# A two-layer cross-attention kernel: the turned context comes from memory instead of from TensorE, and its lower part from GpSimd

## The reference, cut to what matters

```python
# layer 0, for each of the 32 batches
q = Wq y + bq;  k = Wk y + bk;  v = Wv x + bv          # 128 x 1024 each
scores = einsum('bhdl,bhel->bhde', q, k) / sqrt(E)     # 16 x 16 per head
o = Wo (softmax(scores) v) + bo + x
x1 = (o - mean(o)) * rsqrt(var(o) + eps) * gn_w + gn_b
# layer 1: hidden_states = x1, traces = y
q = x1 @ W'q;  k = y @ W'k;  v = y @ W'v               # W' = W + 2 A B
out = x1 + softmax(q k^T / sqrt(32)) v @ W'o           # 32 query heads, 8 key heads
```

## Time and profile before

| | |
|---|---|
| median of 3 runs | 1332.63 us (1332.49 to 1335.76) |
| span of the profiled execution, which is taken for its own time | 1332.9 us |
| TensorE busy | 1321.9 us (99% of the span) |
| VectorE, ScalarE, GpSimd busy | 927.1, 826.5, 150.4 us |
| TensorE's transposes of y (L523) | 256, 34.1 us busy |
| granted TensorE clock | 1.000 |

### The profile page before, as it was taken

The page is one execution under the profiler, slowest core; times in us unless marked ns, Lnnn a source line. Parts: engine busy times, 40 slices in busy tenths (PEclk is TensorE's granted clock), DMA queues, the critical chain, the costliest instruction groups (busy, mean ns, idle before and its releaser), DMA issues.

```text
span 1332.9 us, 23820 instructions
## 1 busy us (share of the span) xinstructions
PE 1321.9 (99%) x7171; PEld 1055.4 (79%) x7171; DVE 927.1 (70%) x2080; ACT 826.5 (62%) x2934; POOL 150.4 (11%) x124
## 2 busy tenths in 40 slices
PE   8999999999999999999999999999999999999999
PEld 7888888888888888888888888766776777766667
DVE  6766666666666777777767776597777677666666
ACT  5766665555541777777757776666666666655441
POOL 5343333222210000000000001400000000000000
PEclk9999999999999999999999999999999999999999
DMA  7466566667757888777778888999999899988882
GB/s 220 147 209 207 202 201 210 221 218 222 241 164 220 232 228 232 226 237 226 222 215 230 228 239 260 271 253 252 264 253 251 247 248 263 256 220 232 235 227 88
DMA packets 194961, 300.42 MB, mean 225 GB/s; under 512 B 26578, under 2 KB 94004, under 8 KB 194324
## 3 DMA queue, kind: packets, MB, share of 16 engines
q1 hardware_dynamic: 194836, 298.90, 77.9%
HBM read 213.88 MB, written 84.93 MB: 224 GB/s over the span
## 4 chain that ended last, share of the span: by engine, by line
PE 95%; DVE 2%; DMA 1%; SPq 1%; issue 1%; ACT 1%; DVEq 0%; ACTq 0%
PE bank L707 26%; PE bank L757 23%; PE bank L586 13%; PE bank L778 8%; PE bank L811 5%; PE bank L822 5%; PE bank L660 3%; PE bank L523 2%; PE bank L572 2%; PE bank L678 2%; PE bank L614 1%; PE bank L693 1%; PE bank L619 1%; PE bank L545 1%; PE bank L633 1%
## 5 line engine op out<-in xcount | busy, mean ns | idle before, releaser
L1058 ACT ACTIVATE bank<-bank,negs 128x128 f32<-128x128 f32 x1024 | 348.3, 341 | 174.8 <-DVE negs L1340 174.4
L707 PE MATMUL bank<-hT,wq 128*128 128x512 f32 x1488 | 390.2, 400 | 0.0
L757 PE MATMUL bank<-wo,op 128*128 128x512 f32 (+1 forms) x1356 | 346.0, 393 | 0.3 <-issue 0.3
L707 PEld LDWEIGHTS bank<-hT,wq 128*128 128x128 f32 x1488 | 264.0, 189 | 46.2
L757 PEld LDWEIGHTS bank<-wo,op 128*128 128x128 f32 x1356 | 249.6, 189 | 52.0 <-issue 1.5
L1335 DVE TENSOR_REDUCE maxes<-bank 128x4 f32<-128x512 f32 x256 | 175.8, 687 | 134.2 <-PE bank L778 134.2
L1075 ACT ACTIVATE probT<-bank 128x512 f32<-128x512 f32 x256 | 152.2, 605 | 112.9 <-PE bank L811 110.1
L1058 ACT ACTIVATION_READ_ACCUMULATOR bank<-bank,negs 128x1 f32 x1024 | 210.0, 205 | 0.0
L586 PE MATMUL bank<-wkv_hi,yT 128*128 128x512 f32 x512 | 200.3, 420 | 0.9 <-DVE wkv_lo L1487 0.7
L778 PEld LDWEIGHTS bank<-k_stack,q_stack 96*128 96x128 f32 x1024 | 150.3, 191 | 17.5 <-issue 1.6
L778 PE MATMUL bank<-k_stack,q_stack 96*128 96x128 f32 x1024 | 147.3, 266 | 1.0 <-issue 0.6
(11 more groups left out here) (172 smaller groups left out, 1629.5 us busy)
## 6 DMA issues: line engine op xcount, KB each, us to landing
q_stack<-q_dram SPq DMA_DIRECT2D x256, 256.0 KB, 4.0
q_dram<-q_part SPq DMA_DIRECT2D x64, 512.0 KB, 4.2
q_stack<-q_dram SPq DMA_DIRECT2D x256, 128.0 KB, 4.3
y_in<-in_ctx SPq DMA_DIRECT2D x32, 512.0 KB, 4.5
x_in<-in_x SPq DMA_DIRECT2D x32, 512.0 KB, 5.1
h_dram<-h_out SPq DMA_DIRECT2D x32, 512.0 KB, 2.7
h_in<-h_dram SPq DMA_DIRECT2D x32, 512.0 KB, 3.9
k_stack<-k_dram SPq DMA_DIRECT2D x128, 128.0 KB, 3.4
```

The source lines that it names most:

```text
L707: m = pe.matmul(bank(u % 2).rearrange("p (a n) -> p a n", a=2), wq[:, block, part, c, :], hT[(group + 1) % 2][:, :, of, c, :], start=c == ...
L757: mm = pe.matmul(place[:, columns], op[m][:, of, c, :], wo[m][w][:, c, columns], start=c == 0 and of == 0 and w == 0, stop=c == GROUP - 1 ...
L1058: act.activation(part, part, ACT.Exp, bias=negs[:, n % RING, j:j + 1], scale=SCORE1, accum_out=sums[:, score_column(k), g, j:j + 1]).then_ ...
```

## The change

The host lays out a second copy of the context, `ctx_turned`, in which the positions of each chunk lie on the partitions. SyncE loads it into `yT_in` (`load_yT`, 512 KB a batch), beside the untouched one, which is still needed for the sums. `turn_y` goes, with its 256 transposes. ScalarE rounds the whole of `yT_in` in one instruction out of SBUF. The lower part of batches 0 and 1 is still made by VectorE (`rest_yT`, now with both inputs in SBUF); that of batches 2 to 31 by GpSimd (`lower_yT(b + 1)` in turn b, 128x1024, both inputs in SBUF, behind the power). TensorE's idle transposes at the start (`keep_on`) become 26 in one piece, and small products on rows of the identity.

```diff
-            def turn_y(b):
-                ...
-                for c in range(NC):
-                    m = pe.transpose(banks[0][:, c * P:(c + 1) * P], y_in[b % 2][:, c * P:(c + 1) * P], ident[:])
+            def wait_yT(b, half):
+                if b < 2:
+                    pe.wait_ge(S["yT_lo"], 2 * b + half + 1)
                 else:
-                    pe.wait_ge(S["const"], CONST["ident"])
+                    pe.wait_ge(S["yT_lo_pool"], b - 1)
...
-            def round_yT(b, half):
+            def round_yT(b, half=None):
...
-                act.wait_ge(S["yT_mm"], 2 * b + half + 1)
-                act.copy(yT_half(b, half, 0), bank(half).rearrange("p (c n) -> p c n", c=4)).then_inc(S["yT_hi"], 1)
+                act.wait_ge(S[f"yT_in{b % 2}"], DMA * (b // 2 + 1))
+                of = yT_chunks(half)
+                act.copy(yT[b % 2][:, of, 0, :], yT_in[b % 2][:, of, :]).then_inc(S["yT_hi"], 1)
...
-                dve.tensor_tensor(yT_half(b, half, 1), bank(half).rearrange("p (c n) -> p c n", c=4),
-                                  f32(yT_half(b, half, 0)), ALU.subtract).then_inc(S["yT_lo"], 1)
+                dve.tensor_tensor(yT[b][:, of, 1, :], yT_in[b][:, of, :], f32(yT[b][:, of, 0, :]),
+                                  ALU.subtract).then_inc(S["yT_lo"], 1)
...
                 norm_scale(b - 1)
-                rest_yT(b + 1, 0)
                 softmax0_end(b)
...
-                rest_yT(b + 1, 1)
...
+            def lower_yT(b):
+                if b >= B:
+                    return
+                pool.wait_ge(S["yT_hi"], 4 + b - 1)
+                pool.tensor_tensor(yT[b % 2][:, :, 1, :], yT_in[b % 2][:], f32(yT[b % 2][:, :, 0, :]),
+                                   ALU.subtract).then_inc(S["yT_lo_pool"], 1)
...
                 if b == 1:
                     stack_lora("o")
+                lower_yT(b + 1)
                 for n in units_of(b)[:-1]:
                     prep_rest(n)
...
             for b in range(B):
+                load_yT(b + 2)
+                load_x(b + 1)
                 load_y(b + 2)
-                load_x(b + 1)
```

More of the change, by code:

```diff
@@ L133, in xattn_two_layers @@
         lora_raw("o")
+        yT_in = [sb(f"yT_in{i}", [P, NC, P]) for i in range(2)]
         at[0] = w_place
@@ L502, in op_part, with yT_chunks @@
             return op[m][:, part, :, :].rearrange("p j n -> p (j n)")
-        def yT_half(b, half, part):
-            return yT[b % 2][:, 4 * half:4 * half + 4, part, :]
+        def yT_chunks(half):
+            return slice(0, NC) if half is None else slice(4 * half, 4 * half + 4)
         def tensor_program(pe):
@@ L673, in turn_h @@
                     pe.wait_ge(S["gram_h"], B)
-                else:
+                elif turn_bank(i) == 2:
                     pe.wait_ge(S["kv"], B)
@@ L829, in keep_on, with keep_on_rows @@
                     pe.transpose(bank(3)[:, 3 * P:4 * P], ident[:], ident[:])
+            def keep_on_rows(n):
+                for _ in range(n):
+                    for r in range(4):
+                        rows = slice(32 * r, 32 * (r + 1))
+                        pe.matmul(bank(r)[:, 0:P], ident[rows, :], ident[rows, :], start=True, stop=True)
             pe.wait_ge(S["const"], CONST["ident"])
-            keep_on(14)
-            turn_y(0)
-            keep_on(4)
+            keep_on(26)
             for half in range(2):
@@ L1043, in round_hT @@
                     act.wait_ge(S[name], B - 1 if i < 4 else B)
-                act.wait_ge(S["yT_mm"], 2 * (B - 1) if i < 4 else 2 * B)
                 act.wait_ge(S["hT_mm"], i + 1)
@@ L1094, in keep_product @@
                 act.copy(c_sb[:, 2, :], out_bank(pair, 0)).then_inc(S["kept"], 1)
+            for half in range(2):
+                round_yT(0, half)
             act.wait_ge(S["lora_in_kv"], LORA_IN["kv"])
             act.copy(lora_b["kv"][:], lora_b3["kv"][:]).then_inc(S["lora_b_hi"], 1)
-            for half in range(2):
-                round_yT(0, half)
             for half in range(2):
@@ L1732, in load_lora_b, with load_yT @@
                                      b).then_inc(S[f"lora_in_{m}"], DMA)
+            def load_yT(b):
+                if b >= B:
+                    return
+                if 2 <= b < 4:
+                    sp.wait_ge(S["yT_lo"], 2 * (b - 1))
+                elif b >= 4:
+                    sp.wait_ge(S["yT_lo_pool"], b - 3)
+                sp.dma_start(yT_in[b % 2][:], ctx_turned[b]).then_inc(S[f"yT_in{b % 2}"], DMA)
             def load_y(b):
@@ L2057 @@
     arrays, args = {}, []
+    ctx = inputs["ctx_4096"]
+    laid = dict(inputs)
+    laid["ctx_turned"] = ctx.reshape(ctx.shape[0], ctx.shape[1], -1, P).transpose(0, 3, 2, 1)
     for name in _INS:
-        a = np.ascontiguousarray(inputs[name])
+        a = np.ascontiguousarray(laid[name])
         arrays[f"in_{name}"] = a
```

36 lines of the change are left out of this document (12 added, 24 removed).

## The result

The changed kernel takes 1353.45 us (median of 4 runs, 1351.71 to 1355.26), the kernel before 1333.16 (4 runs, 1332.49 to 1335.76): 1.0150 times as long, 95% interval 1.0136 to 1.0165. The prediction was 1344, with a range up to 1352, so the time lies above the range. The direction and the mechanism at the product with the attention weights came out as argued; the sum of the other terms, turn 1 above all, is 10 us short. The profiled execution took 1355.26 us, its span 1353.5. Lines of the changed kernel: L1269 is the multiply that was L1276, L620 the product that was L626, L1680 GpSimd's new lower part.

The account below looks back on a forecast made before the run. TensorE's list was taken as the bound. The terms 2.8 - 0.7 + 0.9 + 7.8 - 1.5 + 1.4 = +10.7 on 1332.9 gave 1343.6, taken as 1344 us; own range 1338 to 1350, 8 in 10 from 1331 to 1352.

Parts of the forecast that it names:

- What bounds: First stage: TensorE's list is the bound; a turn's worth is decided at L626, by the chain ending in L1276.
- Do the two disturb each other?: VectorE's multiply L1276 against GpSimd's lower_yT: the multiply waits until GpSimd's 2.39 us instruction ends.
- Turns without a piece, +0.06 each: Turns 2 and 17 to 30, no weight piece: L626 at 253.62 against 253.56, +0.9 us in all.
- Turns with a piece, +0.65 each: Twelve turns with a weight piece ahead of GpSimd's power: lower_yT runs later, L626 0.65 us later, +7.8 us in all.
- Turns 6 and 7, -1.5: Power before the piece: the multiply gets in at the piece's end, ahead of lower_yT, -0.75 us each.
- Turn 1, -0.7: Turn 1, three short GpSimd pieces between: a gain of 0.7 us was taken.
- The start, +2.8: Before turn 1: late y of batch 0 holds ScalarE's list, +2.1, and rest_yT waits for GpSimd, 0.7; range 0 to 3.5 us.
- The DMAs, +1.4: 512 KB more a turn: raw weights land 1.4 us later, late in turn 29 only, up to 3 if others join.
- The rival of late transfers in most turns: Raw weights 0.5 us late in the 15 turns with output pieces, +7.5 us, 1351; chance 0.06.
- The rival of no block, 1315: The multiply doesn't wait for GpSimd, turns 1 to 30 win 0.77 us (0.65 in twelve), 1315 us; chance 0.14.

Follow-up runs that it names:

- e7: The kernel before, transposes kept, plus an extra 128x1024 GpSimd subtraction of two different tiles nobody uses, no second copy: 1351.11 us.
- e1: The changed kernel with GpSimd's lower part cut from one 128x1024 instruction into eight of 128x128: 1328.74 us.
- e11: The changed kernel with one line more: GpSimd's long instruction waits for the attention weights of its turn: 1326.45 us.
- e6: The changed kernel with TensorE filling two long waits, in the first turn and turn 1, with transposes into a bank nobody reads: 1352.00 us.
- e5: The changed kernel, GpSimd's long instruction kept, with order repairs at the start and turn 30 and a GpSimd wait in turn 1: 1347.34 us.
- e8: The kernel before, transposes kept, with a second load of the untouched context into tiles nobody reads: 1338.84 us.
- e3: The changed kernel with the lower part made by VectorE in one instruction behind its multiply, nothing new on GpSimd: 1326.75 us.
- e2: The changed kernel with the multiply of the attention weights on ScalarE instead of VectorE, GpSimd's instruction whole: 1334.37 us.
- e10: The changed kernel with GpSimd's lower part in eight pieces, repairs of the start and turn 30, and a GpSimd wait in turn 1: 1324.84 us.
- e12: The changed kernel with the lower part on VectorE, repairs of the start and turn 30, and y(0) loaded ahead of the layer-0 weights: 1321.02 us.

## Why the prediction was too low, and what in it was right

*What bounds, and "Do the two disturb each other?"* Right, and shown in both directions: e7 puts GpSimd's instruction into the kernel before and gets turns 11 and 20 of the changed one, e1 and e11 take its hold away and win 24.7 and 27 us against the changed kernel. The Trainium skill (SBUF — State Buffer, section SBUF: two separate sides) says that the one that starts first keeps the shared pair of ports for the whole instruction, and that ScalarE's access to SBUF never waits for anyone. The trace agrees on the hold: 1.11 us at the median in place of 0.29 on VectorE, 0.40 on ScalarE with GpSimd at work. Who was first can't be read from the records to a few hundredths of a us: in turn 1 of the changed kernel the multiply's starts 0.02 us ahead of GpSimd's, and it was held.

*Turns without a piece, +0.06 each.* Measured +0.23 on average (turns 2 and 17 to 29: +3.2 together). L620 starts 0.15 us behind the multiply's end (269.08 to 269.23), where I had put 0.05. The next product follows it after 0.22 us, and in turns of before, in which nothing is waited for, after 0.14. These two, 0.10 and 0.08, are the 0.17 that the forecast lacked.

*Turns with a piece, +0.65 each.* Measured +0.77 on average, +9.3 in place of +7.8, most of it the same short times. *Turns 6 and 7, -1.5.* Right: -1.45.

*Turn 1, -0.7.* This is the step that failed most: +2.77. I took a gain there without working out when the multiply falls due against GpSimd's three short pieces. It became ready as the last one ended, GpSimd's long one went first, and it stood 2.44 us. The product came at 9.46 us of the turn in place of 8.16, so the hold is 1.30 of it; the clock's fall behind that is 1.33 (e6), and nothing in the prediction stands for it. In e6, with GpSimd 0.6 us later, the multiply was not held at all, so which way this turn goes hangs on when x of batch 1 lands, which GpSimd's list waits for (0.8 us into the turn in the changed kernel, 1.9 in e6).

*The start, +2.8.* Measured +4.08. The late y(0) is nearly as forecast (sum_y starts at 14.67; y was to land near 14.3), though ScalarE idles for 4.24 us there and not 2. The Gram's copy behind it made TensorE 2.2 us late (17.13 against 14.95). The fall of the clock behind the stop adds 1.27 (e6), and without it the start would have been as forecast. The clock's fall was put at nothing in the sum.

*The DMAs, +1.4.* Turn 30 grew by 2.40. The step named the right transfer; it came 2.1 us late where 0.4 and 1.4 had been put, and again the clock fell behind the stop. e5 removes all of this by the order of issue (11.52). The rival of late transfers in most turns did not occur (e8).

The misses are 3.5 us in turn 1, 1.3 at the start, 2.4 in turns without a piece, 1.5 in turns with one, 0.9 in turn 30 and 0.3 behind it, some 9.9 of the 20.6. Of that 2.6 us are the clock at the start and in turn 1; what its fall cost in turn 30, no run separates. About 4 are the turns with and without a piece, most of it the short times between one engine's end and the next one's start, which count 27 times; 2.1 are the hold in turn 1 in place of the gain that I had put there.

*The rival of no block, 1315.* e11 and e3, in which the multiply takes 0.29 us, gave 1326 and 1327. Their quiet turns win 0.60 to 0.62 us, not 0.77: with the transposes gone the softmax's chain decides, at 6.69 us of the turn, and TensorE's start behind it counts every time.

## What to carry to other kernels

In this kernel, work that went to GpSimd because it is idle was free only where VectorE had no SBUF instruction of the held kind due during it: look at when the longest GpSimd instruction lies against the one VectorE instruction that TensorE waits for, and move it behind that one by a wait (27 us here, for one line), or cut it into pieces. Price a new stop of TensorE with the start behind it (0.15 us here), and count with a fall of its clock, 1.3 us here, if it is as long as the ones above. When every turn gets shorter, look at loads that are issued once a turn, and issue them ahead of the writes in the same queue.

## What the runs showed that I had not expected

- In the first stage most long stops of TensorE come with three to seven us at a granted clock of 0.50: stops of 3.16, 2.03 and 1.81 us in the changed kernel, 2.92 and 1.48 in e1, 2.90 in e2, 2.83 and 3.08 in e3, 1.81 and 2.04 in e5, 2.87 in e8, 1.90 in e10, 2.87 and 2.04 in e11. The length alone doesn't decide: behind 1.97 us in e12, behind 1.69 in turn 3 of the changed kernel, and behind all stops of 1.44 in turns of turn 11's kind the clock stayed at 1.00. In e6, where the engine worked through the first two, it stayed there too. The two falls that can be set against e6 cost 1.27 and 1.33 us, each from one pair of executions.
- Which engine gets in is settled by about 0.1 us (0.02 in turn 1 of the changed kernel, 0.11 in turn 7 of e5), so one late load can turn a gain of 0.6 us into a loss of 4 (e5, turn 7). That may be why e5's runs scatter, between 1345.8 and 1353.8; only the slowest of them has a trace.
- A GpSimd subtraction of 128x1024 takes 1.89 us if its inputs are one tile, and 2.40 if they are two.
